# A transformer layer on one core: the fourth early gate and up chunk is placed in three pieces around the last tiles, and the first down product waits for its banks one by one

## The reference

```
x = x + layernorm(attention(layernorm(x)))      # 16 heads of 32, causal, biases on q, k, v and o
gate, up = split(layernorm(x) @ w_gate_up.T)     # 2 x 2048 columns
x = x + layernorm((silu(gate) * up) @ w_down.T)  # 2048 -> 512
```

## Time and profile before

| | us |
|---|---|
| median of 3 runs | 1033.45 (1031.44 to 1034.08) |
| the profiled execution | 1033.51 |
| its span, first to last instruction | 1031.7 |
| PE busy | 973.6 (94%) |
| DVE, POOL, ACT busy | 718.2, 690.9, 410.5 |
| mean granted TensorE clock | 0.977 of full speed |

### The profile page before, as it was taken

One profiled execution on the slowest core, in us unless ns is written; L12 is line 12 of the kernel. 1 busy time (PEld: TensorE's weight loads), 2 busy tenths in 40 slices (PEclk: granted clock), 3 DMA queues, 4 the chain that ended last, 5 costly groups with the idle time before them and its releaser, 6 DMA issues.

```text
span 1031.7 us, 15426 instructions
## 1 busy us (share of the span) xinstructions
PE 973.6 (94%) x5518; PEld 749.8 (73%) x5518; DVE 718.2 (70%) x1418; ACT 410.5 (40%) x717; POOL 690.9 (67%) x498
## 2 busy tenths in 40 slices
PE   2988999999999999988798999999999999999997
PEld 2766777676676766654576888888888888888886
DVE  6675777887597877875777677776665877777722
ACT  3214545555214545555334333332443433333242
POOL 4203888889635999899165977753688778767273
PEclk9988999999999999988898999999999999999999
DMA  6331333332321333330232311221432322311043
GB/s 215 88 85 48 83 96 86 86 87 73 118 92 37 86 95 83 77 102 26 78 103 97 98 62 64 78 73 42 153 123 92 103 74 77 106 62 62 20 153 133
DMA packets 49181, 90.69 MB, mean 88 GB/s; under 512 B 10448, under 2 KB 10960, under 8 KB 48848
## 3 DMA queue, kind: packets, MB, share of 16 engines
q1 hardware_dynamic: 48560, 89.43, 28.6%
q10 hardware_dynamic: 544, 0.26, 0.1%
HBM read 55.84 MB, written 8.39 MB: 62 GB/s over the span
## 4 chain that ended last, share of the span: by engine, by line
PE 76%; DVE 10%; POOL 7%; ACT 2%; issue 2%; DMA 1%; SPq 1%; POOLq 0%; ACTq 0%; DVEq 0%
PE ps L1647 19%; PE ps L1649 19%; PE ps L1648 19%; PE ps L1727 6%; PE ps L1761 5%; PE ps L1703 5%; POOL p_sum L745 3%; PE ps L1775 1%; DVE ps L1303 1%; DMA x_in<-x 1%; POOL p_sum L748 1%; DVE p_sum L1266 1%; DVE xt_lo L1280 1%; DVE stats L1442 1%; PE ps L1735 1%
## 5 line engine op out<-in xcount | busy, mean ns | idle before, releaser
L1303 DVE CUSTOM_DVE_ANT_0 ps<-ps,mask_q 128x384 f32<-128x384 f32 (+7 forms) x256 | 189.9, 779 | 70.7 <-PE ps L1703 67.4
L1727 PE MATMUL ps<-q_stack,k_stack 98*128 98x512 f32 (+3 forms) x384 | 117.8, 384 | 10.1 <-ACT p_own L980 4.0
L1703 PE MATMUL ps<-k_stack,q_stack 96*128 96x512 f32 (+3 forms) x384 | 110.5, 371 | 3.9 <-DVE m_full L1303 2.6
L767 POOL TENSOR_TENSOR dn_lo<-dn_raw,dn_hi 128x512 fp32r<-128x512 f32 x48 | 66.3, 1382 | 48.0 <-ACT dn_hi L1072 48.0
L1703 PEld LDWEIGHTS ps<-k_stack,q_stack 96*128 96x128 f32 x384 | 68.2, 196 | 31.9 <-DVE m_full L1303 14.0
L1727 PEld LDWEIGHTS ps<-q_stack,k_stack 98*128 98x128 f32 x384 | 63.2, 193 | 35.5 <-ACT p_own L980 8.9
L812 POOL TENSOR_TENSOR gu_lo<-s_raw,gu_hi 128x1024 fp32r<-128x1024 f32 x27 | 64.9, 2402 | 23.2 <-ACT gu_hi L1143 23.2
L980 ACT ACTIVATE p_own<-ps 128x512 f32<-128x512 f32 x112 | 61.0, 598 | 40.7 <-PE ps L1727 23.5
L980 ACT ACTIVATE x_in<-ps 128x512 f32<-128x512 f32 x112 | 60.9, 597 | 36.8 <-PE ps L1727 21.7
L1166 ACT ACTIVATE silu<-ps 128x512 f32<-128x512 f32 x27 | 16.2, 599 | 141.5 <-DVE ps L1538 141.5
L808 POOL TENSOR_TENSOR a_lo<-gu_raw,a_hi 128x512 fp32r<-128x512 f32 x27 | 35.9, 1328 | 51.3 <-ACT a_hi L1136 51.2
(11 more groups left out here) (222 smaller groups left out, 2802.4 us busy)
## 6 DMA issues: line engine op xcount, KB each, us to landing
gu_raw<-gu_w SPq DMA_DIRECT2D x37, 512.0 KB, 3.6
dn_raw<-dn_w SPq DMA_DIRECT2D x48, 256.0 KB, 2.6
x_in<-x SPq DMA_DIRECT2D x32, 256.0 KB, 3.8
q_stack<-st_hi SPq DMA_DIRECT2D x128, 64.0 KB, 2.0
k_stack<-st_hi SPq DMA_DIRECT2D x128, 64.0 KB, 2.0
qk_raw<-qk_w SPq DMA_DIRECT2D x16, 256.0 KB, 3.0
q_stack<-st_lo SPq DMA_DIRECT2D x64, 64.0 KB, 2.0
k_stack<-st_lo SPq DMA_DIRECT2D x64, 64.0 KB, 2.0
```

The lines of the kernel that those rows point to most:

```text
L767: nc.gpsimd.tensor_tensor(dn_lo[:, s], dn_raw[:, s], dn_hi[:, s].bitcast(F32), ALU.subtract).then_inc(dn_split, 1)
L1303: nc.vector.tensor_tensor_reduce(out=scores, in0=scores, in1=mask_q[:, SEQ - (t + 1) * P:], scale=1.0, scalar=MASKED, op0=ALU.add, op1=ALU ...
L1703: last = nc.tensor.matmul(bank[:, 0:width], q_stack[0:QK_ROWS, s, h, t * P:(t + 1) * P], k_stack[0:QK_ROWS, s, h, half * CH:half * CH + wi ...
L1727: last = nc.tensor.matmul(bank[:, at_col:at_col + n * P], k_stack[0:ROWS, s, h, kt * P:(kt + 1) * P], q_stack[0:ROWS, s, h, t * P:(t + n) ...
```

## The change

`AFTER_TILE` now names a chunk and the pieces of it that are placed after a tile. A piece is (part, first k, end k), with part 0 the gate and 1 the up half, and KT = 4. Chunk 3 is no longer placed after T7: its gate half (12 matmuls) comes after T5, the first half of its up part (6) after T6, the second (6) after T7. ACT copies T6 in step 8 ahead of the square root, and T7 between the silus of chunks 0 and 1. DVE's `hidden(0)` and `hidden(1)` both move to step 10, the one ahead of the rest of T7 and the other behind it. PE's wait for all uses of the ring ahead of `down(0)` is replaced by one wait per bank within it: bank t of the four waits for its own last user (T4, T5, T6, T7).

```diff
--- before.py
+++ after.py
@@ -136,7 +136,9 @@
 T_STEPS_AFTER = {("D", 5): (0,), ("D", 6): (1, 2), ("D", 7): (3,), ("D", 8): (4, 5, 6, 7)}
 PER_PAIR, SUMS = 7, 7
 B_SLOTS = 4
-AFTER_TILE = {("O", 3): 1, ("T", 4): 2, ("T", TT - 1): 3}
+WHOLE = ((0, 0, KT), (1, 0, KT))
+AFTER_TILE = {("O", 3): (1, WHOLE), ("T", 4): (2, WHOLE), ("T", 5): (3, ((0, 0, KT),)), ("T", 6): (3, ((1, 0, KT // 2),)),
+              ("T", 7): (3, ((1, KT // 2, KT),))}
 MID = [("V", t) for t, _s in enumerate(V_STEPS) if _s < 0]
 END = []
 for _seq, _lag in ((MID, LAG_T[0]), (END, LAG_T[1])):
@@ -1023,8 +1025,10 @@
 
                 lag = LAG_T[b]
                 for t in range(TT + lag):
-                    if t >= lag:
+                    if t >= lag and (b + 1 < BATCH or t <= TT):
                         hi_of_xt(b, t - lag, use_of("T", b, t - lag))
+                    if b + 1 == BATCH and t == TT:
+                        hi_of_xt(b, t + 1 - lag, use_of("T", b, t + 1 - lag))
                     if t <= TT:
                         slots = range(0 if t < TT else 1, 2 if t else 1)
                         root((2 + 2 * b) * TT + min(2 * t + 1, 2 * TT), slots[0], len(slots))
@@ -1101,8 +1105,9 @@
                     hi_of_tokens(0, t // 2)
                 elif t == TT:
                     act.wait_ge(parked, 2 * PARKED)
-                    for n in range(PARKED):
-                        silus(n)
+                    silus(0)
+                    hi_of_xt(BATCH - 1, TT - 1, use_of("T", BATCH - 1, TT - 1))
+                    silus(1)
                 elif t == TT + 1:
                     hi_of_gu(EARLY_CHUNKS)
 
@@ -1433,8 +1438,12 @@
                         if t == 0:
                             vec.wait_ge(o_bias_loaded, DMA * (b + 1))
                         nc.vector.tensor_tensor(y[:, e % 2, :], ps[:, use % RING], o_bias, ALU.add).then_inc(bank_free, 1)
+                    if b + 1 == BATCH and t == TT + 2:
+                        hidden(0)
                     if t >= lag:
                         lo_of_xt(b, t - lag, use_of("T", b, t - lag))
+                    if b + 1 == BATCH and t == TT + 2:
+                        hidden(1)
                     if b + 1 < BATCH and t in V_STEPS:
                         values(b + 1, V_STEPS.index(t))
                     if second:
@@ -1460,8 +1469,6 @@
                         centred(y[:, e % 2, :], y[:, e % 2, :], 0).then_inc(y_ready, 1)
                     if second:
                         centred(xn[:, e1 % 2, :], x1[:, e1 % 2, :], 1).then_inc(xn_ready, 1)
-                    if b + 1 == BATCH and t > TT:
-                        hidden(t - TT - 1)
 
             vec.wait_ge(consts_loaded, DMA)
             vec.wait_ge(consts_made, 1)
@@ -1835,9 +1842,9 @@
                         transpose_x(2 * TT + b * TT + t, use_of("T", b, t))
                     extra(kind, t)
 
-            def gate_and_up(n):
-
-                s, k = n % 2, plain_of(n)
+            def gate_and_up(n, pieces=WHOLE):
+
+                s = n % 2
                 blk = n // CHUNKS
                 cols = slice(blk * BLK, (blk + 1) * BLK)
                 pe.wait_ge(gu_split, n + 1)
@@ -1846,13 +1853,15 @@
                     pe.wait_ge(acc_out, BT)
                 elif n >= 2:
                     pe.wait_ge(parked if early else h_ready, 2 * (n - 1) if early else n - 1)
-                for part, bank in enumerate((0, 2) if blk else (G_BANK, U_BANK)):
+                for part, k0, k1 in pieces:
+                    bank = (0, 2)[part] if blk else (G_BANK, U_BANK)[part]
                     if n == 0 and part:
                         pe.wait_ge(acc_read, ALL_UNITS)
-                    for k in range(KT):
+                    for k in range(k0, k1):
                         w = slice(k * GU + part * P, k * GU + (part + 1) * P)
                         last = three(ps[:, bank + s], gu_hi[:, s, w], gu_lo[:, s, w], xt_hi[:, 0, k, cols], xt_lo[:, 0, k, cols], k == 0, k == KT - 1)
-                    last.then_inc(gu_full, 1)
+                    if k1 == KT:
+                        last.then_inc(gu_full, 1)
 
             def down(n, first=False, final=False):
 
@@ -1862,6 +1871,8 @@
                 if first and m:
                     pe.wait_ge(acc_out, 2 * BT)
                 for t in range(BT):
+                    if n == 0:
+                        pe.wait_ge(bank_free, USES - (USES - 1 - banks[t]) % RING)
                     cols = slice(t * P, (t + 1) * P)
                     last = three(ps[:, banks[t]], h_hi[:, n % 2, cols], h_lo[:, n % 2, cols], dn_hi[:, m % 2], dn_lo[:, m % 2], first, final)
                 last.then_inc(down_done, 1)
@@ -1944,7 +1955,7 @@
 
             def first_chunks(kind, t):
                 if (kind, t) in AFTER_TILE:
-                    gate_and_up(AFTER_TILE[kind, t])
+                    gate_and_up(*AFTER_TILE[kind, t])
 
             pe.wait_ge(consts_made, 1)
             for kind, t in START:
@@ -1980,7 +1991,6 @@
                     gate_and_up(0)
                     residual(b, END, first_chunks)
 
-            pe.wait_ge(bank_free, USES)
             down(0, first=True)
             down(1)
             gate_and_up(EARLY_CHUNKS)
```

## The result

| | before | changed |
|---|---|---|
| median of 20 runs each, us | 1032.11 (1028.76 to 1034.19) | 1029.37 (1025.36 to 1033.37) |
| ratio, 95% interval | | 0.9972 [0.9960, 0.9984] |
| span of the profiled execution | 1031.7 | 1026.6 |
| T5 to the end of the span | 485.1 | 480.6 |

The change is 2.7 us faster, a difference clear of the measurement but under 0.3%. The profiled execution of it is 5.1 us shorter; 0.6 of that was won ahead of T5 (546.01 instead of 546.57), where nothing was changed, and 4.5 behind it. So the execution in the profile gained more than the median did, and that difference is what the experiments are about.

The account below looks back on a forecast made before the run. PE bounds the kernel: busy all the time behind gate_and_up(4) at 566.40, so only its waits and low clock ahead of that can be won. 1033.5 - 4.7 + 0.2 = 1029.0 us; range 1027.8 to 1033.7.

Parts of the forecast that it names:

- PE's side: PE from T5 to gate_and_up(4): chunk 3's pieces fill two gaps at full clock; gate_and_up(4) at 561.67 instead of 566.40, 4.7 us.
- ACT and DVE: Copy of T6 ahead of the root, which waits for nothing; hidden(0) starts with its silu at 553.35, 1.66 us earlier.
- One wait per bank: PE within down(0): four bank waits in place of one for the ring, worth 0 to 0.6 us, here about 0.1.
- The 0.2 set aside for the added waits: PE's four bank waits and two more changes between transposes and products: a cost of 0.2 us, bounds 0 to 0.5.
- The turns of DVE and POOL: During hidden(0) and hidden(1), DVE and POOL alternate whole instructions; with DVE's turn kept, h_lo of chunk 1 ends at 558.9.
- the product of `hidden(1)` against the third sum: Turn near 556.2 between DVE and POOL, margin 0.03 us, said to decide whether L761 comes ahead of h_lo.
- The first rival: POOL gets the turn at 556.2, PE waits 2.8 before down(1): 1031.1, with low clock 1032.6 to 1033.9, middle 1032.4; chance 0.34.
- the lower of my two bounds: Low clock behind the wait before down(1) in the lost-turn case: 3.4 to 6.8 us long.
- The clock at the new waits: Clock falls behind the 1.65 us wait before down(0) though turns go well: costs 1.6 to 2.4, 1030.4 to 1031; chance 0.13.
- Slower: POOL has its turn, PE waits 2.8 before down(1), clock stays low 6.8 us: gate_and_up(4) at 567.1, time 1034.2; chance 0.06.
- Given back later: DVE's or POOL's work for chunk 5 does not move with PE, so the gain is lost: 1033.4; chance 0.05.

Follow-up runs that it names:

- e3: Only PE's side of the change against the kernel before, ACT and DVE in their old order: 1032.25 us, ratio 1.0001.
- e4: Only ACT's and DVE's new order and one wait per bank against the kernel before, chunk 3 whole behind T7: 1031.96 us, ratio 1.0005.
- e5: e1 with PE's one wait for all uses of the ring ahead of down(0) put back: 1026.47 us, ratio to before 0.9953.
- e1: The changed kernel with POOL waiting for h of chunk 1 before L763: 1027.58 us, ratio to before 0.9958.
- e2: The changed kernel with DVE's h_lo of chunk 1 waiting for POOL's L763: 1033.64 us, ratio to before 1.0011.
- e7: e1 with six products, results unused, in PE's wait ahead of down(0): 1027.90 us, ratio to before 0.9967.
- e9: e1 with the weight loads of chunks 4 and 5 each issued one tile earlier: 1027.60 us, ratio to before 0.9960.
- e10: The changed kernel with POOL's first sum waiting for h_hi of chunk 0, no wait at L763: 1026.89 us, ratio to before 0.9956.
- e6: The changed kernel with POOL's chunk 4 weights behind h of chunk 1 and its four chunk 5 sums behind those: 1027.56 us, ratio to before 0.9961.

## Why the prediction was right, and where it was not

*PE's side.* Right in each start. Forecast behind T5 (546.57 in the trace of before): T7 at 5.69, down(0) at 9.13, down(1) at 12.38, `gate_and_up(4)` at 15.1; measured 5.72, 9.20, 12.43 and 15.29. The waits themselves came out shorter (0.52, 1.43 and 0.19 for 0.8, 1.65 and 0.5), because PE's own pieces took somewhat longer than I had added up. The clock kept 1.00 over the filled gaps. All of it reached the end: 4.54 us at `gate_and_up(4)`, 4.5 at the end of the span, as the row with PE busy all the time had promised.

*ACT and DVE.* Right: the root wasn't held, `hidden(0)` started with its silu, and e3 and e4 show that the earlier h and the earlier PE need each other: in the profiles 1.1 and 0.9 us alone, 4.5 together.

*One wait per bank.* Sized at 0.1, measured 0.11 (e5). The 0.2 set aside for the added waits is the difference between 15.1 and 15.29; no run measures these waits by themselves.

*The turns of DVE and POOL.* The mechanism was right, and the length of each delayed instruction too. The step that failed is which turn decides, and with it the chance. I had put the chance on the product of `hidden(1)` against the third sum, 0.03 us apart. In the profile after, that one went as forecast (555.68 against 555.72), and it stays 0.02 to 0.04 apart, in DVE's favour, wherever the first turn was kept (also in e1, e2, e4, e5 and e7): both sides of it follow from the h_lo before. What decides is the first: h_hi of chunk 0 against the first sum, whose start is a DMA's landing. Of this start the prediction says that it "does not move". It names an earlier landing as a second way to the same loss, but by 0.1 us or more, and gives it no chance of its own. In the traces with the changed order and the old loads (all but e3 and e9), h_hi starts 7.57 to 7.62 behind T5. The first sum, where the landing releases it, starts 7.57 to 7.71 behind T5, so it can come on either side of h_hi. In the three profiles of the changed kernel h_hi and the sum were at 553.60 and 553.72, kept, then at 554.15 and 554.12 and at 554.31 and 554.30, both lost. In e4, where nothing forces a turn either, h_hi was 0.04 ahead and all turns were kept, and in e5 it was ahead by only 0.01, with the same order behind it. e10, which settles this turn by a wait, kept the turns in its profile and has no run above 1029.4.

I gave a lost turn 0.34, as one outcome for the whole kernel; in fact single executions of the same kernel go either way. The share of them can be estimated: with 4.5 us for a kept turn and 0.7 for a lost one (485.1 less 484.3 and 484.5), a mean gain of 2.7 means (4.5 - 2.7) / 3.8 = 0.47. The interval of the ratio, 1.7 to 4.1 us, leaves room for 0.1 to 0.75; two of three profiles lost it.

So the forecast of 1029.0 lies near 1029.37 in part by luck. It counted 4.5 us where 2.7 were measured, 1.8 too much, and started from 1033.5 where 20 runs of before have a median of 1032.1, 1.4 too high; the two errors nearly cancel. The kernels in which the turn is settled do have the forecast gain: their ratios, 0.9953 to 0.9967, are 3.4 to 4.9 us below before.

The Trainium skill (SBUF — State Buffer, "SBUF: two separate sides") has the lock go to whichever starts first, for the whole instruction. The traces agree: when L763 started 0.36 ahead of the last h_lo, that h_lo took 2.73 us instead of 0.69, and POOL had the turn when its sum started 0.01 ahead of h_hi (the third profile), DVE when h_hi was 0.01 ahead (e5).

*The first rival* (turn lost, 1031.1 or, with the clock, about 1032.4) was priced right: its profiled executions took 1032.73 and 1032.96. Its parts were other than I thought: not one wait of 2.8 but 1.98 and 1.84, where a kept turn has 1.43 and 0.19; the low clock of 3.4 us behind them is the lower of my two bounds. Of the 3.75 us, the longer waits are 2.20 and the clock is the rest, about 1.55.

*The clock at the new waits* (0.13): not seen. No profile has a low clock between down(0) and down(1) behind a wait of 1.03 to 2.05, and filling the wait (e7) wins nothing. The clock fell in down(1) behind 1.98 and 1.84 together (2.00 and 1.83 in the third profile) and in e2 behind 3.71; in e3 it fell in down(0), behind 3.85. The length of a wait alone doesn't tell it: in e4 it fell behind the 1.93 ahead of T6, and in e5 it held behind 2.05.

The rule of the Trainium skill on short idles (TensorE: Matmul & The Clock Gate, "A second HAM failure mode: psum-queue depth-cycling"), by which the clock can go down and up, was one of my reasons for this rival. No trace shows it where the turn was kept: the clock stayed at 1.00 from T5 on, also behind three short waits. Where the turn was lost, the clock went down and up once.

*Slower* did not occur in the changed kernel, but e2 forces it: 20.41 against 19.83 behind T5. *Given back later*: not in the changed kernel; e6 shows how it would look.

## What to carry to other kernels

Filling an engine's idle time wins only if what it needs next comes earlier too; look at the wait behind the gap before the gap. Where a profile shows two engines taking turns, list all the turns between them, with the margin of each and what sets it; one whose margin is below a tenth of a microsecond, with a DMA's landing on one side, can go either way from one execution to the next. One semaphore wait that fixes it can be worth more than half of the edit again (here 4.5 us instead of 2.7). And when the profiled execution gains more than the median does, take a second profile of the same kernel: here it showed the other half of the runs.

## What the runs showed of the hardware

In these traces a copy from SBUF to SBUF (h_hi) or an operation with two SBUF operands on DVE took turns with the instructions of POOL. The one that starts second shows its wait as a longer duration: it grows by the rest of the other's instruction, less about 0.14 us (h_hi from 0.43 to 0.98 behind a sum of 0.73, h_lo from 0.69 to 2.73 behind an L763 of 2.54). An operation with one operand in PSUM kept 0.68 beside POOL (L1285, 555.08).

A first sum that started 0.03 us ahead of h_hi, instead of 0.12 behind it, went with an end 3.7 us later, through the turns that follow and the clock.

The time ahead of T5 varied by 5.8 us between executions (542.87 to 548.66), and from the first product of chunk 0 on it was the same within 0.35 (T5 came 41.96 to 42.30 behind it). So this part of the spread is older than the stage that was changed. Much of it is there within the first 85 us. ACT loads a table at that point; this is its row in before and in e10, whose T5 came 3.70 apart:

```profile
84.67 1.28 ACT L1113 ACT_TABLE_LOAD   x1
```

```profile
80.89 1.28 ACT L1119 ACT_TABLE_LOAD   x1
```

They are 3.78 apart already. Over all 14 profiles this load starts between 80.71 and 85.71, and the stretch from it to T5 takes 461.9 to 465.2. In the trace of before the clock is at 0.50 from 52.93 to 56.30; in that of e10 it is at 1.00 from 20 to 70. That the clock is what sets the spread there is a guess: no experiment was made on it. The spread of T5, 5.8 us, is twice the gain of the change, which is why the profiles are compared behind T5.
